# A gated delta-rule layer with a ternary feed forward on one core: the projections of each pair computed one turn sooner

## The reference

```python
q = silu(conv4(x @ Wq.T)); k = silu(conv4(x @ Wk.T)); v = silu(conv4(x @ Wv.T))   # causal, depthwise, 4 taps
beta = sigmoid(x @ Wb.T); g = -exp(A_log) * softplus(x @ Wa.T + dt_bias)
q = l2norm(q) * DK ** -0.5; k = l2norm(k)
def step(S, inp):
    S = S * exp(g)
    v_new = v - k . S
    S = S + beta * outer(k, v_new)
    return S, q . S
o = rmsnorm(scan(step, 0, tokens)) * norm_w * silu(x @ Wg.T)
x = layernorm(x + o @ Wo.T)
x = layernorm(x + ternary(x) @ (ternary(w) + rram).T)
```

## Time and profile before

| | |
|---|---|
| median of 3 runs | 430.26 us (430.23 to 431.33) |
| the profiled execution | 430.67 us, span 428.8 us |
| busy, share of the span: PE, DVE, ACT, POOL | 63%, 75%, 28%, 13% |
| mean granted TensorE clock | 0.76 of full |
| turn 0, from 84.1 to 160.6 us | 76.5 us, DVE busy 60.7 |
| turn 1, from 160.6 to 252.5 us | 91.9 us, DVE busy 73.9 |
| turn 2, from 252.5 to 344.6 us | 92.1 us, DVE busy 75.3 |
| turn 3 and the end, from 344.6 us | 84.2 us, DVE busy 54.4 |

### The profile page before, as it was taken

One profiled execution on the slowest core, in us unless ns is written; L12 is line 12 of the kernel. 1 busy time (PEld: TensorE's weight loads), 2 busy tenths in 40 slices (PEclk: granted clock), 3 DMA queues, 4 the chain that ended last, 5 costly groups with the idle time before them and its releaser, 6 DMA issues.

```text
span 428.8 us, 14040 instructions
## 1 busy us (share of the span) xinstructions
PE 269.3 (63%) x6314; PEld 183.2 (43%) x6314; DVE 322.5 (75%) x790; ACT 119.7 (28%) x245; POOL 56.8 (13%) x63
## 2 busy tenths in 40 slices
PE   3982810698576449795677459785664284986552
PEld 1481600545454217363544336454542263754331
DVE  0765999847698995949798986777989948257996
ACT  0874310056711210356312112357012000232010
POOL 1000360002420200013311100024102000000000
PEclk9965575589777868989676559897686577799686
DMA  7400000000000010000000030000000111000101
GB/s 249 181 0 3 2 0 0 5 2 3 4 3 3 0 50 3 2 3 2 4 3 2 3 98 3 2 3 4 3 2 0 52 50 53 2 5 3 50 0 49
DMA packets 8011, 9.69 MB, mean 23 GB/s; under 512 B 1808, under 2 KB 7056, under 8 KB 7952
## 3 DMA queue, kind: packets, MB, share of 16 engines
q1 hardware_dynamic: 7024, 8.41, 5.9%
q10 hardware_dynamic: 928, 0.39, 0.4%
HBM read 6.70 MB, written 2.10 MB: 21 GB/s over the span
## 4 chain that ended last, share of the span: by engine, by line
DVE 54%; PE 32%; issue 7%; ACT 5%; DMA 1%; DVEq 0%; SPq 0%; ACTq 0%
PE pc L333 7%; PE pj L346 6%; DVE sub_buf L1016 4%; DVE conv_buf L917 4%; PE fr L333 4%; DVE sub_buf L1014 3%; PE pg L457 3%; PE fr L572 2%; PE fr L480 2%; PE pj L457 2%; DVE r_sb L1062 2%; DVE ss L951 2%; DVE stats L1114 2%; DVE r_all L905 1%; DVE t_all L904 1%
## 5 line engine op out<-in xcount | busy, mean ns | idle before, releaser
L917 DVE SCALAR_TENSOR_TENSOR conv_buf<-raw,wconv,conv_buf 128x512 f32<-128x512 f32 x72 | 55.5, 777 | 16.7 <-ACT conv_buf L624 15.1
L346 PE MATMUL pj<-xt,wproj 128*128 128x512 f32 x96 | 54.7, 706 | 8.1 <-DMA xt<-x_t 7.2
L865 POOL TENSOR_TENSOR s_dec<-s_sb,decay 128x192 f32<-128x192 f32 x24 | 14.4, 601 | 216.8 <-DVE s_sb L1071 121.3
L686 ACT ACTIVATE u_sb<-pc 128x192 f32<-128x192 f32 x32 | 10.5, 329 | 114.6 <-PE pc L333 114.6
L333 PE MATMUL pc<-r_sb,t_t 32*32 32x64 f32 x672 | 18.3, 250 | 35.1 <-DVE r_sb L1062 34.3
L333 PE MATMUL fr<-dt_m,chunk_buf 32*32 32x32 f32 x768 | 12.0, 237 | 40.4 <-issue 20.3
L333 PEld LDWEIGHTS pc<-r_sb,t_t 32*32 32x32 f32 x672 | 13.0, 124 | 46.1 <-DVE r_sb L1062 42.8
L346 PEld LDWEIGHTS pj<-xt,wproj 128*128 128x128 f32 x96 | 19.5, 222 | 27.5 <-issue 23.1
L358 PE MATMUL pg<-xt,wproj 128*128 128x512 f32 x48 | 29.3, 739 | 0.0
L333 PEld LDWEIGHTS fr<-dt_m,chunk_buf 32*32 32x32 f32 x768 | 11.2, 151 | 42.0 <-issue 42.0
L457 PE MATMUL pg<-wout,conv_buf 128*128 128x256 f32 x36 | 14.2, 570 | 18.7 <-DVE conv_buf L1108 18.7
(11 more groups left out here) (161 smaller groups left out, 575.8 us busy)
## 6 DMA issues: line engine op xcount, KB each, us to landing
xt<-x_t SPq DMA_DIRECT2D x1, 1536.0 KB, 9.5
x_buf<-x SPq DMA_DIRECT2D x3, 512.0 KB, 3.7
out<-hid_buf SPq DMA_DIRECT2D x6, 256.0 KB, 2.2
wproj<-w_proj SPq DMA_DIRECT2D x1, 1024.0 KB, 8.1
xt<-x_t SPq DMA_DIRECT2D x1, 512.0 KB, 5.9
kq<-x SPq DMA_DIRECT2D x1, 512.0 KB, 3.5
out<-v_tok SPq DMA_DIRECT2D x2, 256.0 KB, 2.1
wout<-w_out SPq DMA_DIRECT2D x1, 384.0 KB, 10.0
```

The lines of the kernel that those rows point to most:

```text
L346: mm = pe.matmul(pj[:, j % 2, :], wproj[:, t, j * P:(j + 1) * P], xt[:, t, k * TOK:(k + 1) * TOK], start=(t == 0), stop=(t == KT - 1))
L686: act.activation(u_sb[:, :, :].rearrange("p g v -> p (g v)"), pc[:, 0:G3 * DV], ACT.Copy).then_inc(u_done, 1)
L865: pool.tensor_tensor(s_dec[:, :, :], s_sb[:, :, :], decay[:, :, c:c + 1].to_broadcast([P, G3, DV]), ALU.mult).then_inc(sdec_done, 1)
L917: e = dve.scalar_tensor_tensor(out=conv[:, d, :, :], in0=raw[:, d, :, m:m + T], scalar=wconv[:, j, m:m + 1], in1=conv[:, d, :, :], op0=ALU ...
```

## The change

All six projections of pair k+2 are computed at the end of turn k: on PE projection 0 after `to_state(5)`, 1 and 3 between `solve` and `to_state` of steps 6 and 7, 2 and 4 behind them, 5 before `merge`. Those of pair 1 are computed in the prologue. ACT's copies out of PSUM go with them. `raw` and `conv` have six buffers each and `o_ch` has its own memory. What DVE, ACT and POOL do for pair k+1 within a turn is laid out anew. On DVE, by the slot in which it stands:

| slot | before | after |
|---|---|---|
| handoff | taps 0 | taps 0, taps 1 (before the first `inverse`) |
| after next_state(0) | taps 1 | taps 2, pair_parameters |
| residual(1) to next_state(1) | taps 2 | taps 3 |
| after next_state(1) | pair_parameters | nothing |
| residual(2) to next_state(2) | feed_forward_sum, taps 3 | kq_to_tokens, feed_forward_sum |
| after next_state(2) | kq_to_tokens | taps 4 |
| residual(3) to next_state(3) | taps 4, moments | taps 5 |
| after next_state(3) | taps 5 | factors |
| residual(4) to next_state(4) | v_to_tokens | moments |
| after next_state(4) | factors | nothing |
| residual(5) to next_state(5) | scaled_operands | v_to_tokens, scaled_operands |
| later | unchanged | unchanged |

The core of the diff:

```diff
-CONV_DEPTH = 4
-SLOT = [(j + CONV_DEPTH - 1) % CONV_DEPTH for j in range(CONV_TILES)]
-        raw = sb("raw", [P, CONV_DEPTH, 2, T + TAPS - 1])
-        conv = view(conv_buf, 0, CONV_DEPTH, 2, T)
+        raw = sb("raw", [P, CONV_TILES, 2, T + TAPS - 1])
+        conv = sb("conv", [P, CONV_TILES, 2, T])
-        o_ch = view(conv_buf, 0, GATE_TILES, TOK)
+        o_ch = sb("o_ch", [P, GATE_TILES, TOK])
...
 # project, on PE
-                    if j == 1:
-                        after(pe, y_in, 0, k - 1, 2)
+                    if j == 1 and k > 1:
+                        after(pe, y_in, 0, k - 2, 2)
...
 # turn, on PE
-                if front and not first(k):
-                    project(k + 1, 0)
+                ahead = k + 2 < PAIRS
...
                     from_state(k, c)
-                    if front and c == 1:
-                        project(k + 1, 3)
                     if tail and c == 2:
                         feed_forward_products(k - 1, 0)
                     if front and 6 <= c < 8:
                         gates(k, c - 5)
                     solve(k, c)
-                    if front and c == 0:
-                        project(k + 1, 1)
                     if tail and c == 1:
                         feed_forward(k - 1)
-                    if front and c == 1:
-                        project(k + 1, 4)
                     if tail and c == 2:
                         feed_forward_products(k - 1, 1)
                     if front and c == 2:
-                        project(k + 1, 5)
-                    if front and c == 3:
                         exponents(k + 1)
                     if front and c == 4:
+                        chunk_products(k + 1, 1)
+                    if ahead and c >= 6:
+                        project(k + 2, 2 * c - 11)
+                    to_state(k, c)
+                    if front and c == 3:
                         chunk_products(k + 1, 0)
-                    to_state(k, c)
                     if front and c == 4:
-                        chunk_products(k + 1, 1)
-                    if front and c == 5:
                         chunk_products(k + 1, 2)
                     if front and c == 5:
                         gates(k, 0)
-                    if front and c == 0:
-                        project(k + 1, 2)
+                    if ahead and c >= 5:
+                        project(k + 2, 2 * c - 10)
+                if ahead:
+                    project(k + 2, 5)
                 if front:
                     merge(k + 1)
...
 # prologue, on PE
-            project(1, 0)
+            for j in range(CONV_TILES):
+                project(1, j)
...
 # turn, on ACT
-                    if front and c == 4:
+                    if front and c == 3:
                         square(k + 1)
...
+                    if ahead and c >= 6:
+                        tile_out_of_psum(k + 2, 2 * c - 11)
                     o_out_of_psum(k, c)
...
+                    if ahead and 5 <= c < 7:
+                        tile_out_of_psum(k + 2, 2 * c - 10)
...
+                if ahead:
+                    for j in (4, 5):
+                        tile_out_of_psum(k + 2, j)
...
 # turn, on POOL
-                    if front and c == 2:
+                    if front and c == 1:
                         g_masked(k + 1)
```

More of the change, by code:

```diff
@@ L616, in tile_out_of_psum @@
                 after(act, proj_done, j + 1, k, CONV_TILES)
-                if not first(k) or j >= CONV_DEPTH:
-                    after(act, silu_done, j + 1 - CONV_DEPTH if j >= CONV_DEPTH else 0, k, CONV_TILES)
-                if not first(k) and j == 1:
-                    after(act, y_mm, 0, k - 1, 2)
+                if not first(k):
+                    after(act, silu_done, 0, k, CONV_TILES)
                 bank = pj[:, j % 2, :].rearrange("p (b t) -> p b t", b=2)
-                act.activation(raw[:, SLOT[j], :, TAPS - 1:], bank, ACT.Copy)
-                act.activation(conv[:, SLOT[j], :, :], bank, ACT.Identity,
+                act.activation(raw[:, j, :, TAPS - 1:], bank, ACT.Copy)
+                act.activation(conv[:, j, :, :], bank, ACT.Identity,
                                scale=wconv[:, j, TAPS - 1:TAPS]).then_inc(tile_out, 1)
@@ L649, in silu @@
                     src = slice(0, 2) if b is None else b
-                    e = act.activation(dst, conv[rows, SLOT[j], src, :], ACT.Silu)
+                    e = act.activation(dst, conv[rows, j, src, :], ACT.Silu)
                 e.then_inc(silu_done, 1)
@@ L674, in merge_out @@
                                    fr[:, n, 0:UH * CH], ACT.Copy).then_inc(p_done, 1)
-            def handoff(k, front):
-                if front and first(k):
-                    tile_out_of_psum(k + 1, 0)
-                merge_out(k)
-                if front and not first(k):
-                    tile_out_of_psum(k + 1, 0)
             def u_out(k, c):
@@ L804, in _ @@
             exp_d(0)
+            for j in range(CONV_TILES):
+                tile_out_of_psum(1, j)
             turn(0, True, False)
@@ L1051, in handoff @@
                     attention_sum(k - 1, 0)
+                if front:
+                    conv_taps(k + 1, 1)
                 inverse(k, 0)
@@ L1242, in turn @@
                     if front and c == 1:
-                        conv_taps(k + 1, 2)
+                        conv_taps(k + 1, 3)
+                    if front and c == 2:
+                        kq_to_tokens(k + 1)
                     if tail and c == 2:
                         feed_forward_sum(k - 1)
-                    if front and c == 2:
-                        conv_taps(k + 1, 3)
                     if front and c == 3:
-                        conv_taps(k + 1, 4)
-                    if front and c == 4:
+                        conv_taps(k + 1, 5)
+                    if front and c == 5:
                         v_to_tokens(k + 1)
@@ L1253, in turn @@
                         end_head_sums(0)
-                    if tail and c == 3:
+                    if tail and c == 4:
                         moments(hid)
@@ L1279, in turn @@
                     if front and c == 0:
-                        conv_taps(k + 1, 1)
-                    if front and c == 1:
+                        conv_taps(k + 1, 2)
                         pair_parameters(k + 1)
                     if front and c == 2:
-                        kq_to_tokens(k + 1)
+                        conv_taps(k + 1, 4)
                     if front and c == 3:
-                        conv_taps(k + 1, 5)
-                    if front and c == 4:
                         factors(k + 1)
```

36 lines of the change are left out of this document (13 added, 23 removed).

## The result

The changed kernel takes 441.37 us (440.61 to 443.11 over four runs) against 430.25 us for the kernel before on the same chip: a ratio of 1.026, with an interval of 1.023 to 1.029. It is slower by 11.1 us. The forecast was 436.0, with a range that ended at 441.5. The sign was right, and the loss is about twice the one that was worked out. The profiled execution took 441.42 us (span 439.6), 10.8 more than the one before.

The account below looks back on a forecast made before the run. DVE was taken to bound the kernel, by its work, gaps and waits. Turn 0 plus 3.0, turn 1 plus 3.1 and turn 2 minus 0.4 gave plus 5.7 on 430.67; with the median 0.4 lower, 436.0 us, range 427 to 441.5.

Parts of the forecast that it names:

- (a): Handoff, middle turns: `conv_taps(k+1,1)` fits into DVE's wait for `project_out`'s second part, minus 2.1 us.
- (b): Step 1, middle turns: with projections 3 and 4 gone from the trip, the wait before `next_state` goes, minus 2.8 us.
- (c): Between `next_state(1)` and `residual(2)`, middle turns: nothing stands there any more, wait 1.0 instead of 0.47, plus 0.5 us.
- (e): `v_to_tokens`, middle turns: moved to step 5, long after the last SiLU, its wait goes, minus 1.5 us.
- (d): Step 2, middle turns: `kq_to_tokens` waits for both feed forward products, 4.1 instead of 1.36 + 1.19, plus 1.55 us.
- (g): Behind `next_state(4)`, middle turns: with `factors` gone to step 3, DVE waits for PE, plus 1.9 us.
- (f): Step 4, middle turns: `moments` between `residual` and `next_state`, wait 1.4 instead of 0.84, plus 0.6 us.
- (h): Middle turns: large POOL operations hold up DVE operations with two SBUF operands at other places than before, plus 1.5 us.
- Rival 2: `factors`: DVE is not held up by `d_masked`, 5.4 us less in three turns, 430.6, no change; chance 0.12.
- Rival 1: Steps 1 to 6: clock stays high, every trip shorter, sum 11.6 us, 424.4; chance 0.2, mostly in part, 425 to 429.
- Rival 3: Whole kernel: work only moves under DVE, whose gaps cover every new wait, 417 us; chance 0.03.
- Rival 4: All bounds bad: `k_decayed` plus 1.0 and (g) 0.7 us in three turns, 441 us; chance 0.1.

Follow-up runs that it names:

- e9: Changed kernel plus unread matmuls on PE in turns 1 and 2, five ahead of `solve(1)` and two at the end of step 0: 438.55 us, ratio 1.016.
- e11: Changed kernel plus four unneeded copies of a small table on DVE ahead of turn 0: 438.83 us, ratio 1.017.
- e12: Changed kernel plus eight unneeded copies of a small table on DVE ahead of turn 0: 441.44 us, ratio 1.022.
- e5: Changed kernel with `chunk_products(k+1,1)` ahead of `solve(4)` on PE and `v_to_tokens` behind `next_state(4)` on DVE: 431.15 us, ratio 1.000.
- e1: Changed kernel with projection 1 ahead of `solve(6)` instead of between `solve(6)` and `to_state(6)`: 433.87 us, ratio 1.007.
- e10: Kernel before with the change's buffers, projections and PSUM copies, all other work in the old order: 429.62 us, ratio 0.996.
- e8: Changed kernel with projections 1 and 2, `chunk_products(k+1,1)`, `v_to_tokens`, taps 4 and ACT's copy of o all moved into other slots: 413.02 us, ratio 0.959.
- e6: Changed kernel with ACT's copy of o in step 1 before the third SiLU instead of behind it: 434.03 us, ratio 1.006.

## Why the prediction was right in sign and half in size

**What bounds it** was read rightly: in turns 1 and 2 DVE's busy time and its waits account for 7.07 of 7.07 and 3.15 of 3.19 us.

**(a), (b), (c), (e).** Handoff: 2.71 of waits went to 0.82, minus 1.9 for minus 2.1. `next_state(1)`: minus 2.8, right. `residual(2)`: 0.98, right. `v_to_tokens` doesn't wait any more, right.

**(d) is the step that failed.** It read the trip from `residual(2)` to the second sum in turn 3 and took 4.1 us. The wait was 7.12 in both turns: 3.0 too little each, 6.0 together, more than the whole of what the forecast missed. The row was of the right operations at another clock: in turn 3 the products took 2.06 and 1.49 us, here 2.74 and 2.29 (1.5 us more), and `solve` between them 0.86 for 0.54 (0.3); 0.86 more was PE's wait for ACT's copy, which stood behind two SiLUs, and turn 3 has none. These make 2.7 of the 3.0. e9 reaches 3.99 with the products at the upper level; e11 and e12 give 4.40 to 7.15 for the same instructions. So two things were missing from (d): the lower level, and ACT's copy on PE's path. What sets the level in this stretch stays open. The prediction named the clock as a rival, but for this wait only upwards; (g) had a price at the lower level, (d) had none.

**What had no term:** `project_out`, the first work of PE in the turn. DVE's first wait there went from 2.50 to 3.36 and from 1.33 to 2.06, 1.6 together. Projection k+1,0 no longer stands at the end of the turn before, PE had been idle for longer, and its first part took 0.86 more. First the kernel before, then the changed one, in turn 1:

```profile
160.77 4.63 PE L457 MATMUL pg<-wout,conv_buf 128*128 128x256 f32 x12 [6.21 <-DVE conv_buf L1108]
```

```profile
162.09 5.49 PE L454 MATMUL pg<-wout,o_ch 128*128 128x256 f32 x12 [8.18 <-DVE o_ch L1090]
```

It is slower work behind an idle stretch, as in (d), at the other end of the turn. Moving work away from an engine was priced as nothing there. This wait too varies: it is 2.19 in e11's turn 1.

**(f) and (g)** came out at 1.46 (1.4) and 1.76 (1.8 to 1.9), and in e5, with the work of these slots moved, nearly all of both goes.

**(h).** Forecast 1.5, measured about 1.4 more DVE time in turn 1. The parts are close too: 1.18 for `g_masked` (0.9), 1.55 for `d_masked` (1.8), and 1.3 saved at `c_masked` by forecast: 1.4 in sum. Rival 2 is out. But the operation held up was another one than named (below).

**The projections ahead** were forecast at 2.8 and 0.7: `next_state(6)` went from 1.02 to 4.20, plus 3.2, and 0.40 came before `residual(7)`: 3.6 for 3.5 in turn 1. This is right as a sum, and e1 shows that the wait belongs to projection 1. As a statement on moving the projections it is too strong: in e10 the same projection in the same place makes that wait 1.75, where PE was busy until 0.89 us before. As far as these executions go, the price belonged to the projection and the emptied step 5 together. It isn't fixed either: the wait was 1.75 in turn 0 of e5.

**Turn 0** waited 13.8 us, not 15.5: 1.2 before `residual(5)` for 1.9, 1.8 for 2.3 over `exponents`, and nothing before `residual(7)` for 0.7, against 4.2 for 3.8 at `next_state(6)`. Turn 3, priced at nothing, gained 0.8.

**The sum of the misses:** 6.0 for (d), 1.6 for `project_out`, minus 1.7 in turn 0 and minus 0.8 in turn 3 make 5.1. The measured loss of 10.8 less the forecast 5.7 is 5.1.

**The rivals.** Rival 1 had the clock high through the steps; the changed kernel shows it at 0.52 where the products run. Rival 3 (the work only moves under DVE) is near what e8 reaches, but not by this change. Rival 4 gave 441, the measured time, by the wrong terms, so that its hit is luck: POOL cost what was forecast, and the excess came from PE.

## What to carry to other kernels

When work is taken out of an in-order queue, ask what that engine does in the slot instead: an empty slot is first a wait for the engine in the ring, and here it often had slower work behind it. Read the price of a stretch from a row of the same operations and the same idle time ahead of it, and keep the price at the other clock level as a bound on both sides. Put the moved work where its engine already stands idle, ahead of the instruction that it waits with and not behind it: in e1 this took a wait from 4.20 to 0.35. Such moves together with work put into the empty slots made the difference between 2.6% slower and 4.1% faster.

## What the runs showed of the hardware

**The clock and short bursts.** In the changed kernel PE was busy for 10.59 of 12.00 us at a granted 0.52. These were bursts of 24 small matmuls and the products behind them, after 5.3 us idle. e6 had the same 5.35 idle and the same first bursts, and was on the fast level 4.9 us after `solve(1)` began; the changed kernel was not before 11 us. What decides between them was not found; e11 and e12 show that the same sequence of instructions meets either level. The Trainium skill (TensorE: Matmul & The Clock Gate, "What's actually happening") says that activity releases the throttle and idleness brings it back. That fits with e9's turn 1. It doesn't say which of two executions of the same instructions gets the upper level.

**GpSimd and a small one-operand operation.** The prediction had said that DVE operations with two SBUF operands are held up by a large POOL operation, and had let the square root's first, one-operand steps pass. The row at 206.97 is a one-operand operation on 24 int32 numbers, and it stood 1.55 us beside `d_masked`; the two-operand one behind it took 0.18, since POOL was done by then. `residual`, which reads PSUM, still ran in 0.36. The Trainium skill (GPSIMD Engine Reference, "1. Specifications") puts the contention down to DVE instructions in a two-port mode or with two inputs in SBUF. That agrees with the rows as far as they go: the second condition doesn't cover this step, and which mode it ran in no row shows.
